# Entry into the second cross attention: three hand-written orders changed (VectorE, GpSimd, ScalarE)

## The reference

```
x = x + linear_attention(layernorm(x), ctx)         # 16 heads
x = x + moe(layernorm(x))                           # top 2 of 8 experts, and a shared expert
x = x + cross_attention(layernorm(x), ctx, mask)    # softmax, 16 heads, its output normed
x = x + ffn(layernorm(x))                           # 256 -> 1024 -> 256, GELU
```

## Time and profile before

| | |
|---|---|
| median of the runs shown | 391.15 us |
| the profiled execution's own time | 391.04 us |
| its span in the trace | 389.1 us |
| PE busy | 367.5 us, 94% |
| DVE busy | 293.6 us, 75% |
| ACT busy | 244.7 us, 63% |
| POOL busy | 219.8 us, 56% |
| the place of the change | about 222 to 246 us after the span's start |

### The profile page before, as it was taken

The page is one execution under the profiler, slowest core; times in us unless marked ns, Lnnn a source line. Parts: engine busy times, 40 slices in busy tenths (PEclk is TensorE's granted clock), DMA queues, the critical chain, the costliest instruction groups (busy, mean ns, idle before and its releaser), DMA issues.

```text
span 389.1 us, 10016 instructions
## 1 busy us (share of the span) xinstructions
PE 367.5 (94%) x3258; PEld 329.5 (85%) x3258; DVE 293.6 (75%) x842; ACT 244.7 (63%) x563; POOL 219.8 (56%) x370
## 2 busy tenths in 40 slices
PE   7799999998999999999999999799999989999996
PEld 6588888786878888989998999688877869999996
DVE  5689988988988879764544499888889995766533
ACT  4576776575554351467876887777877778644550
POOL 3455576378887674604441677577787886531100
PEclk9899999999999999999999999999999999999999
DMA  7561221121332145549784532121120000010101
GB/s 250 187 203 42 79 66 55 40 93 66 87 116 95 70 177 185 161 136 289 232 272 150 192 86 79 50 62 57 54 57 3 2 3 2 7 50 29 56 27 56
DMA packets 31187, 38.13 MB, mean 98 GB/s; under 512 B 4385, under 2 KB 28322, under 8 KB 31138
## 3 DMA queue, kind: packets, MB, share of 16 engines
q1 hardware_dynamic: 28066, 29.11, 24.4%
q0 software_dynamic: 3072, 8.39, 6.4%
HBM read 24.90 MB, written 12.58 MB: 96 GB/s over the span
## 4 chain that ended last, share of the span: by engine, by line
PE 55%; DVE 19%; POOL 12%; issue 8%; ACT 4%; DMA 1%; SPq 0%; ACTq 0%; POOLq 0%; DVEq 0%
PE PS L334 9%; PE PS L335 8%; PE PS L336 8%; PE PS L2266 8%; PE PS L2284 8%; POOL xs_rows L710 3%; PE PS L2101 2%; POOL wfl L482 2%; POOL rj L769 2%; PE PS L2004 2%; ACT raw L1063 1%; POOL rows_early L753 1%; DVE arena_f L1746 1%; PE PS L2342 1%; POOL sj L773 1%
## 5 line engine op out<-in xcount | busy, mean ns | idle before, releaser
L1102 ACT ACTIVATE arena_f<-PS,cols 128x256 f16<-128x256 f32 x64 | 26.5, 472 | 21.6 <-PE PS L2266 19.1
L334 PE MATMUL PS<-wfh,arena_r 128*128 x117 | 35.1, 300 | 2.2 <-DVE arena_r L1602 1.5
L334 PE MATMUL PS<-w0h,arena_r 128*128 128x256 f32 (+1 forms) x96 | 34.8, 363 | 0.6 <-DVE w0l L1189 0.3
L335 PE MATMUL PS<-wfl,arena_r 128*128 x117 | 33.0, 282 | 0.0
L336 PE MATMUL PS<-wfh,arena_r 128*128 x117 | 32.8, 281 | 0.0
L2266 PE MATMUL PS<-arena_r,w1h 128*128 128x256 f32 x128 | 31.2, 284 | 0.0
L335 PE MATMUL PS<-w0l,arena_r 128*128 128x256 f32 (+1 forms) x96 | 31.1, 324 | 0.0
L2266 PE MATMUL PS<-arena_r,w1l 128*128 128x256 f32 x128 | 31.0, 283 | 0.0
L336 PE MATMUL PS<-w0h,arena_r 128*128 128x256 f32 (+1 forms) x96 | 30.9, 322 | 0.0
L488 POOL TENSOR_TENSOR w1l<-raw,w1h 128x384 fp32r<-128x384 f32 (+1 forms) x14 | 12.7, 910 | 29.8 <-ACT w1h L474 29.8
L710 POOL DMA_INDIRECT xs_rows<-rows_early,posi x24 | 24.2, 1010 | 8.9 <-issue 6.7
(11 more groups left out here) (317 smaller groups left out, 1375.4 us busy)
## 6 DMA issues: line engine op xcount, KB each, us to landing
arena_f<-xs_rows SPq DMA_DIRECT2D x39, 128.0 KB, 2.5
ys_rows<-raw SPq DMA_DIRECT2D x19, 256.0 KB, 2.9
raw<-in_w_ffn SPq DMA_DIRECT2D x16, 241.0 KB, 2.7
raw<-in_w_l SPq DMA_DIRECT2D x12, 192.0 KB, 3.1
ctx_raw<-in_ctxT SPq DMA_DIRECT2D x16, 128.0 KB, 2.0
out<-arena_f SPq DMA_DIRECT2D x7, 256.0 KB, 2.1
raw<-in_w_l SPq DMA_DIRECT2D x5, 256.0 KB, 4.4
x<-in_x SPq DMA_DIRECT2D x1, 1280.0 KB, 6.4
```

What stands on the lines that cost most here:

```text
L334: nc.tensor.matmul(out_ap, lh, rh, start=first, stop=False)
L335: nc.tensor.matmul(out_ap, lh, rl, start=False, stop=False)
L1102: nc.scalar.activation(md16[:, g % 2, n, :], PS[:, M_H[n // 2], (n % 2) * D:(n % 2 + 1) * D], ACT.Gelu, bias=cols[:, 2 * KC + n:2 * KC + n ...
```

## The change

Three orders are changed, one instruction group each way; nothing is added and nothing removed.

```
@@ POOL
-            for t in range(3):
+            for t in range(2):
                 gather(t)
             joint_rstd(0)
+            gather(2)
+            joint_rstd(1)
             gather(3)
-            joint_rstd(1)
             gather(4)
             joint_rstd(2)
             gather(5)
@@ ACT
             norm_x(1)
             keys(5)
             normed_in(1)
+            keys(6)
             norm_x(2)
-            keys(6)
             queries(0)
@@ DVE
             ctx_pair_lo(6)
+            entering(0)
             values(2)
-            entering(0)
-            values(3)
             ctx_pair_lo(7)
             entering(1)
+            values(3)
             values(4)
```

## The result

The changed kernel takes 392.55 us in the median of 22 runs (391.56 to 395.0), the kernel before 390.76 in as many on the same chip. The ratio is 1.0048, with a 95% interval of 1.0037 to 1.0060: slower by 1.4 to 2.3 us, a difference that the interval holds apart from zero. The middle of it lies just under the 0.5% (1.96 us) that the prediction took as the least that can be told, and the interval reaches across that; it told 0.48% from none, so the 0.5% was too coarse. The profiled execution took 392.94 us; the one of before took 391.04, so the traces differ by 1.90 us, and 1.9 was forecast.

The account below looks back on a forecast made before the run. PE was taken as the bound, with DVE waiting for it at the stage's end. ACT 0, POOL 0 and PE's gap on values(3) +1.9 us (containing 0.9 on values(2)), added to 391.04, gave 392.9 us; range 391.2 to 394.0.

Parts of the forecast that it names:

- Where the time is decided: End of the keys and values stage: everyone waits for DVE, DVE for PE, PE for nobody; only PE gaps cost time.
- Steps 1 to 3: DVE's entering(0) waits for its gather, so values(2) and values(3) empty late; PE 0.9, then 1.9 us late, not adding.
- Which landing to take: Tile 0's second gather, ahead of entering(0): its own late landing at 227.8 was used, not the typical 226.9.
- the median 2.8: Rival: tile 0's second gather lands on time, at 226.9; +1.0 us, 392.0; chance 0.27.
- Step 4: Later values banks: no third PE gap; values(7) moved out from 244.9, clip(0) at 246.7 instead of 244.79.
- Step 5: POOL's tile 2 deviation at 240.0, ACT's norm at 241.25; covered by DVE's lateness, price 0; 1.2 us without it.
- Step 6: Behind clip(0): every engine follows from it, so the 1.9 us is carried to the end unshortened.
- ACT deciding: Rival: PE does not wait for the banks and ACT's earlier keys count; -0.5 us, 390.5; chance 0.08.
- No effect: Rival: the PE gaps appear but later slots have slack to swallow them; 391.0 us; chance 0.11.
- PE's clock falling in the gaps: Rival: PE's granted clock drops behind its new idle times; +3.3 us, 394.3; chance 0.09, shared with a further gap.

Follow-up runs that it names:

- e1_dve: Kernel before with only DVE's lines of the change (entering(0) ahead of values(2), values(3) behind entering(1)); 392.63 us against 390.70, ratio 1.0050.
- e7_load96: Changed kernel plus 97 already satisfied waits spread over PE's expert blocks; median 393.25 us against 391.22 for the kernel before, ratio 1.0047.
- e8_load96_swap: Changed kernel plus 97 satisfied PE waits and PE making keys(5) ahead of values(4), keys(6) ahead of values(5); 392.14 us, ratio 1.0023 to the kernel before.
- e9_before_load96: Control: kernel before plus 97 satisfied waits spread over PE's expert blocks; 391.57 us, ratio 1.0021 to the kernel before.
- e2_pool_act: Kernel before with only POOL's new order and ACT's exchange, DVE as before; 391.65 us against 390.70, ratio 1.0035.
- e10_act: Kernel before with ACT's exchange alone, on a slower chip; 24.81 us from first values(0) addition to clip(0); ratios of the two such runs 1.0033 and 1.0024.
- e12_act: Kernel before with ACT's exchange alone, on another slower chip; 24.09 us from first values(0) addition to clip(0); ratios of the two such runs 1.0033 and 1.0024.
- e3_v3_back: Changed kernel with values(3) moved back ahead of ctx_pair_lo(7) and entering(1) on DVE; 393.43 us against 390.70 for the kernel before, ratio 1.0063.
- e11_pool: Kernel before with POOL's order alone, on a slower chip; 26.30 us from first values(0) addition to clip(0); ratios of the two such runs 1.0080 and 1.0082.
- e13_pool: Kernel before with POOL's order alone, on another slower chip; 26.58 us from first values(0) addition to clip(0); ratios of the two such runs 1.0080 and 1.0082.

## Why the prediction was right

**Where the time is decided.** Right. PE's last values(7) and then clip(0) are late by what PE lost, and DVE ends PE's two waits.

**Steps 1 to 3, the gather and two banks.** Forecast: DVE starts entering(0) at 227.85, PE values(4) at 231.43 and values(5) at 235.54. Measured: 227.97, 231.48, 235.56. The idle of DVE is 1.53 for 1.4, PE's idle 0.66 for 0.8 and then 0.73 for 1.0. The forecast counted from the instant at which PE's next matmul was due, and so counted the gaps are 0.82 (231.48 against 230.66) and 0.99 (235.56 against 234.57): the trace counts idle from the end of the matmul ahead, which lasts 0.28 us where the next would start after 0.12. Some luck is in the hundredths: entering(0) started 0.12 later than forecast, and the 0.14 from the end of DVE's write to PE's start was 0.06 both times (231.42 to 231.48, 235.50 to 235.56), which took it back. That the second contains the first, 0.87 late and then 1.93 late, is what the starts show. e1_dve shows these steps by themselves, and e7_load96, with e8 and e9, shows that the load is the reason for the landing, which was argued from one row of 0.1 us.

**Which landing to take.** Taken: the gather's own 3.7; left as a rival: the median 2.8. The trace has 3.84. The trace of e7_load96, where the load is elsewhere, has 2.81, and a stage of +0.80 where the rival said +1.0. Both ends were real, and the place decides between them.

**Step 4.** values(7) from 244.98 (244.9), clip(0) at 246.74 (246.7), no third gap. Right.

**Step 5, POOL and ACT.** The instants were right: deviation 2 at 240.06 (240.0), the norm at 241.44 (241.25). The step's own terms, though, give 235.1 + 2 x 2.3 = 239.7 for deviation 2, and how it came to 240.0 is not written. The statement that DVE's lateness covers them was right. The price without cover was put at 1.2 us; e2_pool_act measured 0.81 in the stage. I had made nothing of it beyond a half sentence; the expectation of that run, close to zero, contradicts my own step 5 and was wrong. What failed there is the term "its price is 0" carried from the full change, where it holds, to a kernel without the cover.

**Step 6.** From clip(0) on the 1.9 is carried: 144.36 after, 144.31 before. Right, and the same in six other traces.

**The rivals.** ACT deciding: refuted by the result, which is slower; in e10_act and e12_act ACT's exchange alone shows no gain either. No effect: refuted. PE's clock falling in the gaps: not in the profiled execution of the change, where 230 to 243 us stand at 1.00, but I was too sure of where such a fall could come from (see below); of the 22 runs of the change one, at 395.0 us, has a mean clock of 0.987 where the others have 0.995 or more, and may have had such a fall; two more, at 394.68 and 394.8, have 0.996, the profiled execution's own. No trace was taken of these three, so what made them long is open.

## What to carry to other kernels

Moving work of a busy engine ahead of a bank's release is paid by the engine that wants the bank, and its price is read off in the trace before: the moved instruction's readiness, the release shifted by it, the other engine's demand. Where several chains run side by side, the price of an edit is not zero because it is covered in one combination; take the cover away in thought and write down the next chain's number, since every cure for the first chain lands on it. Measure such an edit from a fixed instant ahead of the stage to one behind it: 22.62 us came out twice for the same orders here (the kernel before and e9_before_load96), while the median of e7_load96 said +2.0 us for a stage of +0.80. And look for what a cure costs by itself, as in e8_load96_swap, before the rest is put down to the change.

## What the runs showed of the hardware

**An instruction load is a transfer like others.** One of 0.02 MB holds one of 16 DMA engines for about a microsecond (63.8% and 73.6% of 16 engines in 0.1 us are 1.02 and 1.18 us), and a gather under way at that time landed 1.0 us later (3.84 against 2.81). Adding 24 instructions ahead did not move it; 97 did, to 1.3, 1.7 and 2.0 us behind T0 in three traces, instead of 3.1 to 3.5. The Trainium skill (DMA: Bandwidth & Descriptors, Queues, rings and completion order) says that a DMA engine finishes a whole packet before it turns to its next queue; the pair of landings agrees with it, at this one place.

**PE's clock falls behind shorter idles than the rival assumed.** In e2_pool_act PE stood 1.41 us before scores(0) at 244.29 and 0.96 us at 246.78. Its stretches from 243 to 246 and from 247 to 250:

```profile
243.00:246.00 3.00, 1.53 (x18) 1.20 (x18) 2.28 (x6) 3.00 (x8) 2.33 (x5) 1.00 0.30 87
247.00:250.00 3.00, 3.00 (x20) 2.54 (x19) 2.35 (x7) 1.26 (x2) 2.12 (x4) 0.51 0.30 87
```

The granted clock was 0.51, the 1.2 GHz level, in the second; the changed kernel has 1.00 in the same stretch:

```profile
247.00:250.00 3.00, 1.96 (x20) 1.58 (x21) 2.93 (x8) 1.64 (x3) 0.72 (x1) 1.00 0.33 87
```

The rest behind clip(0) was 145.71 us there, 1.40 over the 144.31. e3_v3_back has the same, 1.27 and 0.96 us of idle, a clock of 0.50 from 248 to 251, and 145.66 us. The kernel before stands 0.50 and 0.96 us in these two places. The change does not wait at scores(0); it stands 0.96 us in the second place (247.36) and 0.68 at 249.57. The clock of both holds. So a chain that gets late at scores(0) can pay twice, once in the stage and once behind it. It does not do so in every execution: of the 12 runs of e2_pool_act eight, at 390.71 to 392.08 us, have a mean clock of 0.996 to 1.000, and four, at 393.03 to 394.57, one of 0.990 or 0.991; the profiled execution is one of the four. With an idle of 3.11 us (e11_pool, e13_pool) scores(0) itself is slow already.

**Chips differ.** The kernel before took 390.7 to 391.2 us in the median on the chips of the other runs, and 401.87 and 402.57 us on the two of e10_act to e13_pool, while PE's busy time in e12_act is nearly that of the kernel before on the other chips (369.3 us in its first 397 us, 367.5). The excess is idle time, some of it put on no engine of the core, like the 2.27 and 1.00 us above; its cause stays open.
